# TensorE takes the expert slots in pairs: two first products, then two second products

## The reference

```python
x = x + conv0(ln(x))            # x@W_in, state space: KV = sum B (V*dA); y = C KV + V*D; layer norm; @ W_out
t = t + ffn0(ln(t))             # E = 8 experts, hidden 128, top 2 of a softmax gate
x = x + conv1(ln(x))            # x * rsqrt(8x8 channel mix of x^2 + 3x3 neighbours of x^2 + beta) * gamma + beta
t = t + ffn1(ln(t))             # E = 8 experts, hidden 256, top 2 gate

def ffn(xf):                    # dense: every expert is computed for every token
    for e in range(E):
        h = gelu(xf @ W1[e] + b1[e])
        out = out + cw[:, e:e + 1] * (h @ W2[e] + b2[e])
```

## Time and profile before

| | |
|---|---|
| timed runs, us | 718.56 median of 3 (715.98 to 719.94) |
| profiled execution | 720.34 us, span 718.6 us |
| PE busy | 579.9 us, 81% of the span |
| DVE busy | 493.4 us, 69% |
| ACT busy | 372.9 us, 52% |
| POOL busy | 282.1 us, 39% |
| PE H, line 850 | 229.2 us |
| PE Y, line 864 | 215.6 us |
| ACT GELU, line 689 | 210.4 us |

### The profile page before, as it was taken

The page is one execution under the profiler, slowest core; times in us unless marked ns, Lnnn a source line. Parts: engine busy times, 40 slices in busy tenths (PEclk is TensorE's granted clock), DMA queues, the critical chain, the costliest instruction groups (busy, mean ns, idle before and its releaser), DMA issues.

```text
span 718.6 us, 8222 instructions
## 1 busy us (share of the span) xinstructions
PE 579.9 (81%) x2818; PEld 222.5 (31%) x2818; DVE 493.4 (69%) x888; ACT 372.9 (52%) x440; POOL 282.1 (39%) x240
## 2 busy tenths in 40 slices
PE   2325674679897998899998999899989987985976
PEld 1213233342332433243323333433333322321311
DVE  3244357867797879887988798879877883375212
ACT  2113612556566466846585658566755563443532
POOL 2122156134434363535452555265435432234013
PEclk9999965688999899999999999999999997998889
DMA  3500600062206050515041503250325023500320
GB/s 67 102 3 1 133 1 0 15 121 71 49 0 134 6 116 15 115 22 118 16 97 38 120 16 84 50 119 16 64 56 119 15 59 62 119 15 2 71 63 15
DMA packets 27833, 41.37 MB, mean 58 GB/s; under 512 B 11792, under 2 KB 19088, under 8 KB 27792
## 3 DMA queue, kind: packets, MB, share of 16 engines
q1 hardware_dynamic: 27152, 38.75, 26.1%
q0 software_dynamic: 640, 2.10, 1.0%
HBM read 38.22 MB, written 2.62 MB: 57 GB/s over the span
## 4 chain that ended last, share of the span: by engine, by line
DMA 26%; DVE 26%; PE 23%; issue 9%; POOL 6%; SPq 5%; ACT 5%; POOLq 0%; DVEq 0%; ACTq 0%
DMA WB<-w_scratch 22%; PE yP L864 8%; PE hP L850 7%; DVE nacc L1125 6%; DMA w_scratch<-wTs 4%; SPq L401 3%; PE sA L777 3%; POOL stat_c L483 2%; POOL stat_b L483 2%; DVE YW L1172 2%; DVE xnrm L954 1%; PE sC L722 1%; SPq L439 1%; DVE gt L1012 1%; DVE xcen L938 1%
## 5 line engine op out<-in xcount | busy, mean ns | idle before, releaser
L689 ACT ACTIVATE H<-hP,b 128x1024 f32<-128x1024 f32 x192 | 210.4, 1112 | 117.1 <-PE hP L850 116.0
L864 PE MATMUL yP<-H,w 128*64 128x512 f32 x768 | 215.6, 644 | 21.3 <-DVE ACC L1172 20.1
L850 PE MATMUL hP<-xT,w 64*128 64x512 f32 x768 | 229.2, 677 | 1.6 <-ACT H L689 1.6
L553 POOL TENSOR_TENSOR ACC<-ACC,YW 128x512 f32<-128x512 f32 x96 | 125.7, 1313 | 192.1 <-DVE YW L1172 191.9
L850 PEld LDWEIGHTS hP<-xT,w 64*128 64x128 f32 x768 | 61.5, 195 | 104.3 <-issue 83.5
L1172 DVE SCALAR_TENSOR_TENSOR YW<-yP,b,WB 128x512 f32<-128x512 f32 x96 | 71.4, 745 | 31.6 <-PE yP L864 31.4
L864 PEld LDWEIGHTS yP<-H,w 128*64 128x64 f32 x768 | 40.8, 140 | 162.8 <-issue 139.8
L1125 DVE SCALAR_TENSOR_TENSOR nacc<-PAD,taps,nacc 128x256 f32<-128x256 f32 x112 | 60.5, 540 | 3.7
L1172 DVE SCALAR_TENSOR_TENSOR ACC<-yP,b,WB 128x512 f32<-128x512 f32 x32 | 23.1, 747 | 54.5 <-DMA WB<-w_scratch 54.5
L537 POOL TENSOR_SCALAR nrg<-nacc,go_col 128x512 f32<-128x512 f32 x8 | 12.7, 1586 | 68.1 <-ACT nacc L658 68.1
L575 ACT ACT_TABLE_LOAD x23 | 29.5, 1283 | 8.5 <-DVE nacc L1125 6.8
(11 more groups left out here) (137 smaller groups left out, 737.6 us busy)
## 6 DMA issues: line engine op xcount, KB each, us to landing
WB<-w_scratch SPq DMA_DIRECT2D x32, 1024.0 KB, 10.0
X<-in_x SPq DMA_DIRECT2D x8, 256.0 KB, 12.0
out<-X POOLq DMA_DIRECT2D x8, 256.0 KB, 2.8
w<-in_L_ffn_W SPq DMA_DIRECT2D x3, 512.0 KB, 5.4
w<-in_L_ffn_W SPq DMA_DIRECT2D x3, 256.0 KB, 3.7
w_scratch<-wTs SPq DMA_DIRECT2D x16, 32.0 KB, 1.8
mix<-in_L_conv_gamma_k SPq DMA_DIRECT2D x16, 0.2 KB
win_f<-in_L_conv_W_in SPq DMA_DIRECT2D x2, 42.0 KB, 2.5
```

What stands on the lines that cost most here:

```text
L553: pool.tensor_tensor(ACC[l][:, cols], ACC[l][:, cols], YW[:, u % 4, :], ALU.add).then_inc(summed, 1)
L689: nc.scalar.activation(H[:, s % RING, :], hP[s % 2][:, :], ACT.Gelu, bias=b1[l][:, e * ch + c:e * ch + c + 1])\
L850: mm = nc.tensor.matmul(hP[s % 2][:, hf * HALF:(hf + 1) * HALF], w1[l][rows, w, :], xT[l][g % 2][rows, :], start=True, stop=True)
L864: mm = nc.tensor.matmul(yP[hf][a * C:(a + 1) * C, :], w2[l][:, (2 * j + a) * ch + c, :], H[:, (2 * ch * j + 2 * c + a) % RING, hf * HALF:( ...
```

## The change

In PE's list alone, `moe` is split into `hidden` (H) and `expert_out` (Y). At an even slot s of a group it issues H of s, H of s + 1, Y of s and Y of s + 1; at an odd slot nothing. The tables of steps are as before, and so are the lists of the other engines.

```diff
@@ -832,7 +832,7 @@
                     pe.wait_ge(*c_read("send", g))
                     gate_transpose(1, g, sC)
 
-            def moe(m, s):
+            def hidden(m, s):
                 l, g = m
                 ch = CHUNKS[l]
                 if s < E * ch:
@@ -851,6 +851,9 @@
                                               xT[l][g % 2][rows, :], start=True, stop=True)
                     mm.then_inc(h_ready, 1)
 
+            def expert_out(m, s):
+                l, g = m
+                ch = CHUNKS[l]
                 unit = y_unit(m, s)
                 if unit:
                     j, hf, c = unit
@@ -866,6 +869,14 @@
                                               start=(c == 0), stop=(c == ch - 1))
                     if c == ch - 1:
                         mm.then_inc(y_ready, 1)
+
+            def moe(m, s):
+
+                if s % 2 == 0:
+                    hidden(m, s)
+                    hidden(m, s + 1)
+                    expert_out(m, s)
+                    expert_out(m, s + 1)
 
             def final(m, half):
 
```

## The result

| us | before | after |
|---|---|---|
| timed runs | 717.27 median of 4 (713.18 to 719.94) | 737.22 median of 4 (736.48 to 740.75) |
| profiled execution, span | 718.6 | 736.2 |
| ahead of the first send1 | 170.3 | 161.7 |
| first to last send1 | 502.9 | 534.2 |
| behind the last send1 | 45.4 | 40.3 |

The ratio is 1.029, with an interval from 1.023 to 1.036. Each ratio in this document counts the fast runs only; slow are two runs of experiment 9 (717.25 and 712.57 us), two of experiment 11 (719.46 and 718.85) and one of the kernel before beside them (723.64), which stand only in the medians and ranges. The forecast was 734 us. The sum came out; the table shows that its parts did not: the middle lost 31.3 us, the two ends gained 13.7.

What follows compares the result with a forecast made beforehand. PE sets the pace from send1 to layer 0's gate, chains through DVE, ACT and POOL from there to `state`. Six periods of +2.7 us (+16) and -0.5 us for the last group, on 718.6, gave 734 us; range 732 to 751.

Steps and rivals of the forecast that it cites:

- What the change saves: On PE, a further H or Y costs 0.86 us: 0.35 us saved per pair, 4.2 us in a period.
- rival (d): A further Y is not cheaper: Y after Y costs 1.01 us, +11 us, 745 us; chance 0.03.
- Leg 1: From send1 to `turn_a`: new waits for ACT's copies and GELUs, +2.6 us in a period.
- Leg 2: From `turn_a` to layer 0's gate product: pairs save 2.8 us, new waits on ACT outweigh it, +0.3 us.
- rival (c): The clock falls: one more low stretch of 1.5 us in each period, +9 us, 743 us; chance 0.17.
- Legs 3 and 4: Layer 0's gate to `proj1`, then to `state`: ends set by chains through DVE and POOL, 0 and +0.1 us.
- bound of 1.7 us: Upper bound from `proj1` to `state`: `state` starts 1.7 us later if the chain behind `proj2` keeps its 10.4 us.
- Leg 5: From `state` to send1: PE work less 0.7 us, plus 1.3 us waiting for DVE's weights, -0.3 us in all.
- The sum: Over the kernel: +2.7 us in each of 6 periods, +16 us, last group -0.5 us: 734 us.
- Prologue: chain-bound, 0: The prologue is bound by chains and has no pairs to speak of, so it changes by 0.
- (a): The saving wins if the waits on ACT sum to less than 3.2 us a period: 699 us; chance 0.12.
- (b): Nothing changes: half of the waits on ACT are covered, -0.2 us a period, 717 us; chance 0.13.

Runs made afterwards that it cites:

- experiment 9: Changed kernel with pairs only at the ends (shifted: eight slots behind the first send1 paired, eight behind the last not), before's order between: 706.92 us, ratio 0.988.
- experiment 11: Kernel before with 12 and 6 f16 products of no use in the prologue's waits of 4.20 and 2.65 us: 716.02 us, ratio 0.998.
- Experiments 3: Changed kernel with ACT's copies moved to where PE now makes their steps: 722.78 us, ratio 1.012.
- experiment 4: Changed kernel with DVE's scaling put ahead of the top-2 chain of layer 1's gate: 729.94 us, ratio 1.022.
- experiment 5: Changed kernel with both ACT's copies and DVE's scaling moved in their tables: 714.03 us, ratio 1.000.
- experiment 7: Changed kernel with 8 f16 products of no use before `state`, while PE waits for the values: 735.59 us, ratio 1.029.
- experiment 6: Kernel before, without pairs, with DVE's scaling put ahead of the top-2 chain in its table: 751.88 us, ratio 1.055.

## Why the forecast came out

**What the change saves: right.** H H 1.99 and Y Y 1.94 us between other work. With that rival (d) falls, and with it, for this kernel, the rule of the Trainium skill that it stood on (TensorE: Matmul & The Clock Gate, Part 3, The mechanism): by the rule the second Y would have cost 1.01 us more (the price of an alternating one), Y Y 2.09 us. By the rows the saving lies where the kind of tile changes: H H Y Y has two changes in two slots, the alternation four. The Trainium skill (TensorEngine Tiling (Array Packing), Key Properties) says that a change of the tiling mode drains the engine; 0.35 us for two changes fewer agrees with it, but no run here tests it by itself.

**Leg 1: right.** 28.9 us (322.09 to 351.00), forecast 28.5. (The 0.1 us for a semaphore was read too low: 1.21 - 1.02 in the earlier trace rows is 0.19 us. It did little, as the waits of 1.06 us for a forecast of 1.2 show.)

**Leg 2: right on the waits, too low on the clock.** 13.5 us, forecast 11.8. The waits were 1.06 and 1.75 us. The rest is the H H at 359.06: 3.59 - 1.99 = 1.6 us at the lower level. That is rival (c), at 1.5 us a stretch.

**Legs 3 and 4: right.** 7.6 us (forecast 7.9) and 13.2 us (13.1); DVE and POOL set these ends, as said. `proj2`'s delay cost nothing, and of the bound of 1.7 us nothing came.

**Leg 5: the step that failed.** 17.2 us, forecast 14.2. The working took this leg as PE's work plus one wait, 1.3 us at send1. That wait was 0.98 us. But it had asked only which of DVE's steps moved, and none did; it had not asked which of them PE now reaches too soon. Slot 9's Y waits 1.57 us for a scaling behind the top-2 chain. Another 3.54 - 1.99 = 1.55 us are the lower clock behind `state`. Together 3.1 us, less the 0.3 us saved at send1: 2.8 of the 3.0 us missed.

**The sum: two errors against each other.** That the total came within 3 us is luck. A period of 80.5 us and not 75.6. Of the 31.3 us over all gaps the forecast had 15: its six periods count half of one ahead of the first send1. Experiments 3 and 4 price two causes of the loss, the waits for ACT's order (12 us; 16.2 us of the gaps) and for DVE's (5 to 7 us; 8.6 us of the gaps), and with 5 both together are 25.0 of the 31.3 us. At the ends the trace has -13.7 us against a forecast of +0.9 (half a period, 1.4, and -0.5 for the last group); experiment 9, in timed runs, has -9 us for the prologue with a part of the rest. "Prologue: chain-bound, 0" was wrong, since the chain there runs over PE's products behind a wait, at half the clock. Behind the last send1 the forecast had the pairs' saving, 1.8 us of the 5.1; there too before worked at the lower level behind its wait of 3.88 us, and after did not behind one of 1.79:

```profile
689.17 1.98 PE L864 MATMUL yP<-H,w 128*64 128x512 f32 x4 [3.88 <-DVE ACC L1172]
```

```profile
711.94 1.94 PE L867 MATMUL yP<-H,w 128*64 128x512 f32 x8 [1.79 <-DVE ACC L1183]
```

**The rivals.** (a) and (b) fall: ACT's waits sum to 0.30 (behind send1) + 1.06 + 1.21 + 1.06 + 1.75 = 5.4 us a period; (a) needed less than 3.2, and (b) half of 5.9. (c) holds for its place and price. The period of after had a mean granted clock of 0.96, against 1.00 in the period before of the earlier trace rows (columns: stretch, us, busy us of PE, PEld, DVE, ACT and POOL, then PEclk, DMA share, GB/s):

```profile
322.10:402.60 80.50, 67.20 (x353) 27.11 (x353) 60.45 (x109) 46.34 (x55) 35.01 (x29) 0.96 0.29 60
```

```profile
320.90:393.80 72.90, 66.59 (x354) 24.80 (x352) 62.75 (x109) 46.59 (x55) 35.07 (x29) 1.00 0.31 67
```

This pair is the widest apart: the first five gaps had 0.96, 0.98, 1.00, 0.98 and 0.98 before and 0.94, 0.96, 0.96, 0.96 and 0.98 after. The two low stretches were 3.1 us of this period's loss of 7.6. I gave the forecast without (c) 0.55 and (c) 0.17; the time lies between them, and what was measured is both (c) and the unforeseen wait, less the ends. Over all gaps the clock was 0.96 before, 0.95 after and 0.94 in experiment 5, whose gaps are 25 us shorter than after's: what the two tables took back is no difference of the mean clock. What stays open is how much of the rest the clock makes on its own, the middle's last 6.3 us and the pairs' saving that does not show: experiment 7 could move a low stretch, but not take it away.

## What to carry to other kernels

When the order of one engine's list changes, go through every other engine's list at that place and ask of each step that frees a buffer: what stands ahead of it, and does the reordered engine now ask earlier? The same table edit on DVE was worth -0.8% in one order of PE (experiment 4; the intervals overlap) and +5.5% in the other (experiment 6), so fit the lists to each other and move them together. When an experiment switches a change on for a part of the kernel, look in its trace for where the switch fell: here it lay eight slots behind the place that was meant. And cut a trace into prologue, periods and tail before you believe a sum that fits.

## What the runs showed of the hardware

A wait under 2 us can be followed by the lower clock: the H H after 1.75 us took 3.59 us, while in the same kernel the Y after 1.86 us took 1.08. Filling one wait with work moved the low stretch to a later wait (experiment 7), and filling most of a 4.20 us wait delayed and shortened it (experiment 11). A small step of DVE that takes 0.22 us took 1.34 us in the rows above (313.11, line 990), while a step of POOL ran (line 513, from 313.11 on, 1.26 us). That is 1.1 us of the way to the scaling that slot 9's Y waits for, but it is not new: before, two such steps took 0.68 and 1.19 us beside the same step of POOL. What held them was not tested.
